# Layer norm through batch-norm statistics, and a low-rank product in fp16 halves

## The reference, cut to what matters

```python
def _L2_cond_ref(hidden_states, language_ids, W1, b1, W2, b2, gamma, beta):
    h = relu(hidden_states @ W1[language_ids] + b1[language_ids])      # 512 -> 128
    x = hidden_states + h @ W2[language_ids] + b2[language_ids]         # 128 -> 512
    mean, var = mean(x), mean(square(x - mean))
    return (x - mean) * rsqrt(var + 1e-5) * gamma[language_ids] + beta[language_ids]

def _L3_cond_ref(x, language_ids, lora_A, lora_B, lang_embed):
    return (x @ A.T) @ Bm.T + emb                                       # rank 16

x = x + _L0_cond_ref(x, fside, ...)          # attention, 16 heads
x = x + _L1_cond_ref(x, fside, fside, ...)   # attention, one head
x = x + _L2_cond_ref(x, itok_B_0_8, ...)     # adapter with layer norm
x = x + _L3_cond_ref(x, itok_B_0_3, ...)     # rank 16
```

## Time and profile before

| What | us |
|---|---|
| median of 3 runs | 1403.95 (1402.32 to 1405.69) |
| the profiled execution, whole | 1404.92 |
| its span in the trace | 1402.9 |
| PE busy | 1308.7 |
| DVE busy | 934.7 |
| ACT busy | 878.7 |
| POOL busy | 430.1 |

### The profile page before, as it was taken

One profiled execution on the slowest core, in us unless ns is written; L12 is line 12 of the kernel. 1 busy time (PEld: TensorE's weight loads), 2 busy tenths in 40 slices (PEclk: granted clock), 3 DMA queues, 4 the chain that ended last, 5 costly groups with the idle time before them and its releaser, 6 DMA issues.

```text
span 1402.9 us, 19927 instructions
## 1 busy us (share of the span) xinstructions
PE 1308.7 (93%) x7009; PEld 560.5 (40%) x7009; DVE 934.7 (67%) x1594; ACT 878.7 (63%) x1853; POOL 430.1 (31%) x372
## 2 busy tenths in 40 slices
PE   5798999899999999999998999999999999999995
PEld 1332364324543255332553335432454324533252
DVE  6286548874588646985569754896458864688544
ACT  2398545885468833887348864588536884388731
POOL 5341016510363105331064301651035310533114
PEclk8899999999999999999999999999999999999997
DMA  4222002130121302203012300313012130220200
GB/s 142 82 56 75 26 32 73 41 108 1 45 65 43 100 1 62 75 19 97 31 47 60 85 31 31 76 39 108 1 46 65 42 101 1 60 77 17 70 1 31
DMA packets 62161, 75.82 MB, mean 54 GB/s; under 512 B 14378, under 2 KB 35174, under 8 KB 62062
## 3 DMA queue, kind: packets, MB, share of 16 engines
q1 hardware_dynamic: 62062, 74.54, 18.7%
HBM read 40.81 MB, written 8.40 MB: 35 GB/s over the span
## 4 chain that ended last, share of the span: by engine, by line
PE 63%; ACT 19%; DVE 14%; issue 3%; DMA 1%; POOL 1%; SPq 0%; ACTq 0%; POOLq 0%
PE bank L441 23%; PE banks L441 12%; ACT banks L734 9%; DVE nmx L974 8%; ACT big L786 7%; PE bank L1319 6%; PE banks L1303 6%; PE bank L1164 6%; PE banks L1237 3%; PE bank L1266 2%; PE bank L1329 1%; PE bank L1271 1%; PE bank L1293 1%; DVE prod L964 1%; DVE y L1020 1%
## 5 line engine op out<-in xcount | busy, mean ns | idle before, releaser
L974 DVE TENSOR_REDUCE nmx<-banks 128x1 f32<-128x512 f32 x512 | 326.1, 684 | 71.8 <-PE banks L1237 70.7
L734 ACT ACTIVATE banks<-banks,nmx 128x512 f32<-128x512 f32 x512 | 340.1, 670 | 53.0 <-DVE nmx L974 50.4
L786 ACT ACTIVATE big<-banks 128x1024 f32<-128x1024 f32 x256 | 247.2, 1022 | 44.0 <-PE banks L1303 42.9
L441 PE MATMUL bank<-fT,w_hi 128*128 128x512 f16 x768 | 244.3, 379 | 1.1 <-issue 1.1
L1237 PE MATMUL banks<-KQ 97*128 97x512 f16 x512 | 154.3, 383 | 35.2 <-ACT banks L734 33.1
L516 POOL TENSOR_TENSOR big<-x,b2r 128x512 f32<-128x512 f32 x32 | 40.5, 1266 | 415.4 <-DVE x L909 375.3
L1303 PE MATMUL banks<-KQ 98*128 98x512 f16 x512 | 141.0, 382 | 13.7 <-ACT big L786 8.7
L441 PE MATMUL bank<-fT,w_lo 128*128 128x512 f16 x384 | 145.8, 380 | 0.0
L477 POOL TENSOR_TENSOR half<-qk,ones 128x512 f16<-128x512 f32 x64 | 66.5, 1039 | 238.6 <-ACT qk L716 238.6
L1319 PE MATMUL bank<-big,V 128*32 128x512 f32 x1024 | 136.4, 605 | 0.0
L441 PEld LDWEIGHTS bank<-fT,w_hi 128*128 128x128 f16 x768 | 74.8, 97 | 91.6 <-issue 15.3
(11 more groups left out here) (142 smaller groups left out, 1992.5 us busy)
## 6 DMA issues: line engine op xcount, KB each, us to landing
KQ<-half SPq DMA_DIRECT2D x384, 64.0 KB, 2.0
tiles_in<-in_x_dram SPq DMA_DIRECT2D x32, 256.0 KB, 7.3
tiles_in<-in_fside_BxSxS_dram SPq DMA_DIRECT2D x32, 256.0 KB, 2.7
x<-in_x_dram SPq DMA_DIRECT2D x8, 1024.0 KB, 5.7
out_dram<-x SPq DMA_DIRECT2D x32, 256.0 KB, 2.0
w<-in_L_cond_W_dram SPq DMA_DIRECT2D x16, 256.0 KB, 4.7
b2r<-in_L_cond_b_dram SPq DMA_DIRECT2D x8, 256.0 KB, 4.4
gr<-in_L_cond_gamma_dram SPq DMA_DIRECT2D x8, 256.0 KB, 5.6
```

Of the source, the lines that this page charges most:

```text
L441: mm = eng.matmul(out_ap, pairs[n][0], pairs[n][1], start=(first and n == 0), stop=(last and n == len(pairs) - 1))
L734: ins = eng.activation(bank(step, i)[:, j % 2, :], bank(step, i)[:, j % 2, :], ACT.Exp, bias=nmx[:, t, h:h + 1], accum_out=esum[:, t, h:h ...
L786: eng.activation(big[:, n % 2, 2 * u:2 * u + 2, :], bank(step)[:, :, :], ACT.Exp).then_inc(read(step), 1)
L974: eng.tensor_reduce(nmx[:, t, h:h + 1], bank(step, i)[:, j % 2, :], AX_X, ALU.max, negate=True).then_inc(max_done, 1)
```

## The change

The layer norm takes DVE's batch-norm instructions: a new step STAT does bn_stats over the tile, bn_aggr, an addition of epsilon, and (y - mean) * gamma in one fused operation; POOL raises the variance to the power -0.5; NORM is one fused DVE operation, y * rstd + x1. SQ on ACT, the 15 operations, L943 and both POOL operations of SCALE are gone. Statistics go tile by tile, not two tiles at a time.

The low-rank product takes fp16: rows of A are loaded twice, B's columns are stored as high and low half, ACT copies the high half of the LOW result and DVE subtracts to get the low half, and LORA is two fp16 matmuls that accumulate. The embedding row is loaded onto all partitions (`er`, in `t1`) and POOL adds it to x1 in step LOW. Both step lists are written anew. The diff, cut to its core:

```diff
-        adapters = [("X2T", 0), None, ("HID", 0), None, ("ADP", 0), None, ("X2T", 1), ("SQ", 0), ("HID", 1), ("ADP", 1),
...
+        adapters = [("X2T", 0), None, ("HID", 0), None, ("ADP", 0), ("STAT", 0), ("X2T", 1), None, ("HID", 1), ("NORM", 0),
+                    ("ADP", 1), ("STAT", 1), ("X3T", 0), None, ("LOW", 0), ("NORM", 1), ("X2T", 2), None, ("LORA", 0), None,
+                    ("HID", 2), None, ("X3T", 1), None, ("ADP", 2), ("STAT", 2), ("LOW", 1), None, ("X2T", 3), ("NORM", 2),
+                    ("LORA", 1), None, ("HID", 3), None, ("X3T", 2), None, ("ADP", 3), ("STAT", 3), ("LOW", 2), None,
+                    ("LORA", 2), ("NORM", 3), ("X3T", 3), None, ("LOW", 3), None, ("LORA", 3)]
...
+            + [("X2T", 0), ("P1T", 3), ("HID", 0), ("X2T", 1), ("PV1", 2), ("ADP", 0), ("STAT", 0), ("HID", 1), ("PV1", 3),
+               ("NORM", 0), ("ADP", 1), ("STAT", 1), ("X2T", 2), ("X3T", 0), ("NORM", 1), ("HID", 2), ("X2T", 3), ("LOW", 0),
+               ("X3T", 1), ("ADP", 2), ("STAT", 2), ("HID", 3), ("LORA", 0), ("LOW", 1), ("ADP", 3), ("NORM", 2),
+               ("STAT", 3), ("LORA", 1), ("X3T", 2), ("NORM", 3), ("LOW", 2), ("X3T", 3), ("LORA", 2), ("LOW", 3),
+               ("LORA", 3)])
...  POOL
+                    elif step[0] == "HID":
+                        eng.tensor_tensor(x1[:, t, :], x1[:, t, :], br[:, :], ALU.add).then_inc(xg_done, 1)
+                    elif step[0] == "STAT":
+                        eng.wait_ge(var_done, i * NT + t + 1)
+                        eng.tensor_tensor(rstd[:, t % 2:t % 2 + 1], var_eps[:, t % 2:t % 2 + 1], mhalf[:, :], ALU.pow
+                                          ).then_inc(rstd_done, 1)
+                    elif step[0] == "LOW":
+                        wait_full(eng, ("X3T", t), i)
+                        eng.tensor_tensor(x1[:, t, :], x1[:, t, :], er[:, :], ALU.add).then_inc(emb_added, 1)
...  SP
+                for n in range(2):
+                    eng.dma_start(small[n * RANK:(n + 1) * RANK, :],
+                                  lora_A[bass.ds(rlang, 1), :, :].rearrange("a r n -> (a r) n")).then_inc(prep_in, 16)
-                wait_read(eng, ("PREPB",), i)
-                eng.dma_start(lowB[RANK:RANK + 1, :], lang_embed[bass.ds(rlang, 1), :]).then_inc(emb_in, 16)
+                eng.wait_ge(att_f32, i * NG + NG)
+                eng.dma_start(er[:, :], lang_embed[bass.ds(rlang, 1), :].to_broadcast([P, D])).then_inc(emb_in, 16)
...  ACT
-                    elif kind == "SQ":
-                        eng.activation(junk[:, t % 2, :], y[:, t % 2, :], ACT.Square, bias=st[:, t % 2, 1:2],
-                                       accum_out=st[:, t % 2, 2:3]).then_inc(sq_done, 1)
+                        eng.activation(lowT[:, t % 2, 0, :], bank(step, i)[:, 0:P], ACT.Copy).then_inc(low_hi, 1)
...  DVE
-                        eng.scalar_tensor_tensor(out=y[:, t % 2, :], in0=bank(step, i)[:, :], scalar=1.0,
-                                                 in1=xb[:, t % 2, :], op0=ALU.mult, op1=ALU.add,
-                                                 accum_out=st[:, t % 2, 0:1]).then_inc(read(step, i), 1)
+                        eng.tensor_tensor(y[:, t % 2, :], bank(step, i)[:, :], xb[:, t % 2, :], ALU.add
+                                          ).then_inc(read(step, i), 1)
+                    elif kind == "STAT":
+                        eng.bn_stats(stats[:, t % 2, :], y[:, t % 2, :]).then_inc(stat_done, 1)
+                        eng.wait_ge(stat_done, i * 2 * NT + 2 * t + 1)
+                        eng.memset(stat_gap[:, :], 0.0)
+                        eng.bn_aggr(mean_var[:, t % 2, :], stats[:, t % 2, :]).then_inc(stat_done, 1)
+                        eng.wait_ge(stat_done, i * 2 * NT + 2 * t + 2)
+                        eng.tensor_scalar(var_eps[:, t % 2:t % 2 + 1], mean_var[:, t % 2, 1:2], EPS, None, ALU.add
+                                          ).then_inc(var_done, 1)
+                        eng.scalar_tensor_tensor(out=y[:, t % 2, :], in0=y[:, t % 2, :], scalar=mean_var[:, t % 2, 0:1],
+                                                 in1=gr[:, :], op0=ALU.subtract, op1=ALU.mult).then_inc(centred, 1)
                     elif kind == "NORM":
-                        norm_piece(step[1], step[2], i)
+                        eng.scalar_tensor_tensor(out=x1[:, t, :], in0=y[:, t % 2, :], scalar=rstd[:, t % 2:t % 2 + 1],
+                                                 in1=x1[:, t, :], op0=ALU.mult, op1=ALU.add).then_inc(x3_done, 1)
+                    elif kind == "LOW":
+                        eng.wait_ge(low_hi, i * NT + t + 1)
+                        eng.tensor_tensor(lowT[:, t % 2, 1, :], bank(step, i)[:, 0:P], lowT[:, t % 2, 0, :], ALU.subtract
+                                          ).then_inc(read(step, i), 1)
...
+                        eng.wait_ge(emb_added, i * NT + t + 1)
...  PE
-                        eng.matmul(bank(step, i)[:, :], lowT[:, step[1] % 2, :], lowB[:, :], start=True, stop=True
-                                   ).then_inc(done(step, i), 1)
+                        for half_ in range(2):
+                            mm = eng.matmul(bank(step, i)[:, :], lowT[:, step[1] % 2, half_, :], lowB[:, :],
+                                            start=(half_ == 0), stop=(half_ == 1))
```

More of the change, by code:

```diff
@@ L186, in plan_banks @@
     for step in order_mid(True, False):
-        if step[0] not in ("NORM", "SCALE", "SQ"):
+        if step[0] not in ("STAT", "NORM"):
             give(2, step)
@@ L197, in order_last @@
 def order_last():
-    norm = {t: [("NORM", t, n) for n in range(NORM_PIECES)] for t in (0, 2)}
     cut = ORDER_L1.index(("PV1", 1)) + 1
     return ([step for step in ORDER_L1[:cut]]
[L202 to L207, removed]
+            + [("X2T", 0), ("P1T", 3), ("HID", 0), ("X2T", 1), ("PV1", 2), ("ADP", 0), ("STAT", 0), ("HID", 1), ("PV1", 3),
[3 more added lines that the diff above has]
+               ("LORA", 3)])
 def plan_last():
@@ L768, in mid @@
                         wait_full(eng, step, i)
-                        eng.activation(lowT[:, t % 2, :], bank(step, i)[:, 0:P], ACT.Identity,
-                                       bias=ident[:, RANK:RANK + 1]
-                                       ).then_inc(read(step, i), 1)
+                        eng.activation(lowT[:, t % 2, 0, :], bank(step, i)[:, 0:P], ACT.Copy).then_inc(low_hi, 1)
             def attention(i):
@@ L789, in attention @@
                 wait_full(eng, ("PREPB",), i)
-                eng.activation(lowB[:, :], lone[2][:, :], ACT.Copy).then_inc(read(("PREPB",)), 1)
+                eng.activation(lowB[:, :], lone[2][:, 0:D // 2].bitcast(F16), ACT.Copy).then_inc(read(("PREPB",)), 1)
                 wait_full(eng, ("PREPA",), i)
@@ L851, in _ @@
             eng.memset(norms16[:, :, :], 0.0).then_inc(rows_ready, 1)
-            eng.memset(small[:, :], 0.0).then_inc(rows_ready, 1)
-            eng.memset(smallb4[:, :, :, :], 0.0).then_inc(rows_ready, 1)
-            eng.wait_ge(consts, 3)
+            eng.wait_ge(sel_ready, 1)
+            eng.tensor_copy(ident16[:, :], ident[:, :]).then_inc(rows_ready, 1)
             for j in range(NJ):
@@ L1062, in attention @@
             def attention(i):
-                eng.wait_ge(prep_in, i * 48 + 48)
-                for c in range(ND):
-                    eng.tensor_copy(smallb4[:, :, c, 0:RANK], smallb[:, :, :]).then_inc(copied, 1)
+                eng.wait_ge(prep_in, i * 64 + 64)
+                every = smallb[:, :, :].rearrange("p d (c r) -> p d c r", c=1).to_broadcast([P, ND, ND, RANK])
+                eng.tensor_copy(smallb4[:, :, :, 0:RANK], every).then_inc(copied, 1)
+                eng.wait_ge(copied, i * 2 + 1)
+                eng.tensor_tensor(smallb4[:, :, :, RANK:2 * RANK], every, smallb4[:, :, :, 0:RANK], ALU.subtract
+                                  ).then_inc(copied, 1)
                 take_norms(0, i)
```

113 lines of the change are left out of this document (38 added, 75 removed).

## The result

The changed kernel takes 1430.6 us (median of four runs, 1430.4 to 1430.9) where the kernel before takes 1404.5 on the same chip. The ratio is 1.0188, with a 95 per cent interval of 1.0170 to 1.0205: 26 us slower. Forecast were 1410 and a range of 1385 to 1427. The sign was right, the size was 6 instead of 26 us, and the time lies outside the range.

The account below looks back on a forecast made before the run. PE bounds slots 0 to 24, PE, DVE and ACT together the SMAX part, a DVE-POOL chain the last item. Seven passes x (1.3 + 1.2 + 0.4 - 0.2) = +19, -10, -3: net +6, 1410 us, range 1385 to 1427.

Parts of the forecast that it names:

- Slots 0 to 24: First part of each pass, PE-bound: PE work from 7.04 to 8.34 us, 1.3 us longer a pass.
- Nothing else should stall there: Slots 0 to 24: STAT 0 has about 9 us before X3T 0 needs it, its work about 4 us.
- The sum on DVE: Slots 25 to 56: DVE's work falls from 52.6 to 50.1 us, 2.5 us less a pass.
- 3 us of room: Slots 25 to 56: PE's added work falls from 8.8 to 5.7 us, so PE is not the limit.
- The wait in LOW: Slots 25 to 56: DVE stands 1.2 us for ACT's high half, three times a pass, 3.7 us.
- The first rival: SMAX part: LOW's wait costs nothing, as DVE waits for a bank anyway; 1387 us, chance 0.29.
- The lock: Fused DVE operations of STAT and NORM meeting POOL on the shared port: 1.0 us a pass, 0.4 counted.
- The rival that used this rule: Second rival: each fused operation pays a whole POOL operation, or bn_stats takes two passes; 1425 us, chance 0.18.
- Waits fall into each other: Seven passes: some of the added waits coincide, 0.4 us off a pass, -3 us in all.
- the sign turns: LOW's wait: the change comes out faster once more than 1.3 of the 3.7 us is hidden.
- The last item: Last item, chain on DVE: last LORA read at 1389 instead of 1399.8, 10 us earlier; bounds 6 and 12.
- The third rival: Last item doesn't get shorter, as if POOL's power were over 1 us; 1419 us, chance 0.08.

Follow-up runs that it names:

- pool_short: Changed kernel with POOL's additions of beta and of the embedding row cut to one column of 512; 1421.1 us.
- later_and_short: Changed kernel with the edits of low_later and pool_short together; 1415.5 us.
- low_later: Changed kernel with DVE's low half of LOW 1 to 3 moved behind the next slot's SMAX maxima; 1415.6 us.
- later_shift4: As low_later, with all adapter steps of a pass four slots later; 1399.4 us.
- shift4_spread: As later_shift4, with the centring taken out of STAT and put two slots later, except in the last item; 1387.7 us.
- norm_old_low_new: Kernel before, with its norm and order, but the change's low-rank product: fp16 halves, low half on DVE, embedding row added on POOL; 1430.2 us.
- power_cheap: Changed kernel with POOL's power replaced by a product of the same two columns; 1429.0 us.

## Why the prediction was wrong in size

**Where the 20 us lie.** Forecast were +8.2 us in the stages (the -3 in it), +7.7 between them, -10 in the last part and nothing ahead of the first score matmul, +6 in all. Measured were +23.4, +12.9, -8.6 and -1.4. So 15 of the missing 20 are in the stages and 5 between them.

**Slots 0 to 24.** The 1.3 us of moved PE work was right: the shift took it away with the stall. "Nothing else should stall there" was a step that failed. I had checked the time between STAT 0 and X3T 0, and not what stands ahead of X3T 0's copy in DVE's queue: STAT 1 with its centring beside POOL. 0.7 us a pass, 5 in all. I also counted only these slots and not what stands between the last score matmul and them: there LORA 3 gave back 0.9 and waits for DVE and ACT took 0.7.

**The sum on DVE.** I wrote 52.6 before and 50.1 after and booked 2.5 us of gain, and this is the step that failed in the stage. One stage by engine, before and after:

```profile
394.50:451.00 56.50, 52.12 (x272) 21.50 (x271) 50.19 (x95) 49.52 (x143) 26.57 (x24) 1.00 0.20 52
```

```profile
745.90:805.40 59.50, 50.72 (x266) 20.30 (x265) 49.85 (x86) 48.83 (x140) 24.79 (x23) 1.00 0.18 47
```

Before it was 50.19: I had priced the old norm's small operations and reads too high by 2.4 us (one of the eight reads, LORA 3's, lies behind the stage). One look at this view, which was to be had, would have shown it. The 50.1 meets the 49.85 by luck, for 1.1 of that is the held NORM; pool_short, without it, is busy 48.8. So the gain was 0.3 with the lock and 1.4 without, where I had 2.5. With PE the same: 3 us of room were forecast and 1.4 were there.

**The wait in LOW.** Forecast three times 1.2, 3.7 us; seen three times 1.1, 3.3. Its size was right. On the path were 1.1 us with NORM 2 free (pool_short to later_and_short), and 2.2 for wait and held NORM together (low_later). The first rival, that a free slot of DVE hides it, was wrong as a whole; two thirds hidden would fit the 1.1.

**The lock.** 0.4 a pass was mis-sized. In the stage it was 1.1 (pool_short: 59.2 to 58.1), in the slots before it the 0.7 at LOW 0 above: 1.8. Not all of the lengthening costs time: per item NORM took 4 x 0.54 and the centring 4 x 0.17 more than alone, 2.9 us. The Trainium skill, "SBUF — State Buffer", section "SBUF: two separate sides", says that whichever of the two starts first has the shared pair for its whole instruction. The trace agrees: NORM at 411.58 ended when 1.26 of POOL and its own rest were over. The rival that used this rule named the mechanism and 1425. It charged all four operations at the same price; in the stage one of the four was held, and ahead of it one centring counted because X3T 0's copy was queued behind it.

**"Waits fall into each other", minus 3.** With measured sizes my own sum is -0.3 + 3.3 = 3.0 a stage (the held NORM is in the -0.3) against the 3.1 seen, with nothing to take off. Its size is near, its way isn't. Taken away one after another, NORM 2's hold gave 1.1 us a stage (pool_short), the wait in LOW 1.1 (later_and_short), four slots of shift 0.4 though DVE did 1.0 more (later_shift4), and the centring's place 0.7 at the same work (shift4_spread): 55.9, just under the 56.1 before. In another order the shares would differ. That a stage's length depends on where DVE's blocks stand, and not on their sum alone, was in no term of the forecast.

**Slips in the sums.** 32 x 1.29 is 41.3 and not 41.5, and PE's additions after are 5.8 and not 5.7; neither matters. With the -3 in the sum the sign turns where 0.8 of the 3.7 us is hidden, not 1.3.

**Small terms.** bn_stats 0.65 forecast, 0.69 measured; STAT 1.9, measured 0.69 + 0.18 + 0.06 + 0.15 + 0.74 = 1.8; the fp16 transposes -0.2, and -0.2 in the first "between" of norm_old_low_new (110.3 against 110.5; the other six hold new waits of 0.9 for DVE's maxima and are 110.9); the power 0.3, measured 0.55 to 0.99, off the path in the stage and worth 0.4 a pass between the stages (power_cheap).

**The last item.** DVE in the kernel after, ADP 0 and the last LORA (compare):

```profile
1400.05 0.69 DVE L981 TENSOR_TENSOR y<-bank,big 128x512 f32<-128x512 f32 x1
...
1425.66 0.69 DVE L1016 TENSOR_TENSOR x<-bank,x 128x512 f32<-128x512 f32 x1 [1.13 <-PE bank L1277]
```

25.6 us apart against 34.6: 9.0 gained where I had 10, and 8.6 by the last part. The third rival was wrong though the power takes nearly 1 us: with the product in its place the last part is shorter by 0.4 only (109.5 against 109.9, power_cheap).

## What to carry to other kernels

Where several engines hand a few buffers around, do not price a stage by one engine's sum: lay out the blocks in which an engine does anything but the handing-around, and look for the longest, with every wait and every held operation in it. Split such steps and put them in different slots before judging the instructions themselves. A change with its gain in one part and its loss in another can be applied to the first alone, and a bad placement can hide a good instruction: here the same operations gave +26 us as they came and -19 us when spread, shifted and reordered. And an edit meant for one wait also moves who meets whom on the shared port: read the lengths of the operations again before giving it a price.

## What the runs showed of the hardware that I had not expected

A power of 128x1 on POOL takes 0.99 us when it starts beside DVE's centring and 0.55 at the least, against 0.19 for an addition of the same size (pool_short). A product of that size takes 0.63 beside the centring and 0.19 elsewhere (power_cheap), the same 0.44 more. The centring that started 0.16 before the power kept its 0.74 us.

A short stop of PE can be followed by a low clock. PE in the kernel after, in the pass from 228.4 on, and the stretch behind it (last columns: granted clock, DMA share, GB/s):

```profile
243.17 0.87 PE L1222 MATMUL banks<-KQ 97*128 97x512 f16 x2 [1.82 <-ACT banks L742]
```

```profile
243.50:246.50 3.00, 3.00 (x13) 2.28 (x12) 1.82 (x3) 3.00 (x9) 0.00 (x0) 0.50 0.53 149
246.50:249.50 3.00, 3.00 (x17) 1.57 (x16) 1.83 (x3) 1.81 (x5) 1.43 (x2) 0.95 0.08 29
```

The clock stands at 0.50, the 1.2 GHz level, for about 3 us, and the stage is 60.7 instead of 59.2. The same stop of 1.8 us stands in the next pass without such a fall, so it comes in some passes only; in later_shift4 two passes have it at 2.4 us each. Nor does the length of the stop decide it: in later_and_short, whose longest is 1.2 us, two passes have the fall, and in shift4_spread, with one of 1.25, none. Why one and not the other, no run here tells, and so the 4.8 us that shift4_spread got from it may be luck of the placement.
